# A four-batch decoder kernel: the scan's B rows replicated by SBUF-to-SBUF transfers instead of matmuls and copies, later requests for expert weights, and new interleaving tables

## What is computed

```python
deltaA  = exp(einsum('bld,dn->bldn', delta, A))
deltaBu = einsum('bld,bln,bld->bldn', delta, B, u)
h = h * dA_t + dBu_t                 # over l = 0..255, for each d, n
y = einsum('bdn,bn->bd', h, C_t)     # + u * D afterwards
```

## Time and profile before

| | us |
|---|---|
| median of 3 runs | 985.33 |
| lowest, highest | 984.05, 987.88 |
| the profiled execution's own time | 984.03 |
| its span, first to last instruction | 982.2 |

### The profile page before, as it was taken

How to read it: one execution, slowest core, us unless ns; L and a number is a source line. 1 busy time by engine, 2 the same in 40 slices (tenths; PEclk the granted TensorE clock), 3 DMA queues, 4 the chain that set the end, 5 groups by cost and what they waited for, 6 DMA issues and landing times.

```text
span 982.2 us, 13012 instructions
## 1 busy us (share of the span) xinstructions
PE 870.8 (89%) x4643; PEld 652.0 (66%) x4668; DVE 643.3 (65%) x1378; ACT 383.9 (39%) x828; POOL 358.9 (37%) x393
## 2 busy tenths in 40 slices
PE   6897675988999998889999998888999998789997
PEld 5675344754787786744787886653788786426886
DVE  6332799795355998895355999875355999764333
ACT  4111743326236443426326443417226544243111
POOL 5202485120042875220043875220042876000322
PEclk9897877999999999999999999979999999879999
DMA  6204000002023330301024330302022330300452
GB/s 217 110 0 175 0 1 0 1 14 98 1 81 113 126 113 2 107 29 82 1 81 145 97 111 1 108 1 110 1 68 69 94 109 17 108 1 1 129 153 84
DMA packets 22196, 67.69 MB, mean 69 GB/s; under 512 B 2860, under 2 KB 4780, under 8 KB 21492
## 3 DMA queue, kind: packets, MB, share of 16 engines
q1 hardware_dynamic: 21876, 66.80, 20.8%
q10 hardware_dynamic: 256, 0.07, 0.0%
HBM read 65.74 MB, written 1.05 MB: 68 GB/s over the span
## 4 chain that ended last, share of the span: by engine, by line
PE 49%; DVE 19%; POOL 12%; issue 12%; ACT 7%; DMA 1%; ACTq 1%; POOLq 0%; DVEq 0%; SPq 0%
PE B L779 22%; PE F L779 21%; POOL arena L465 7%; DVE arena L1430 5%; DVE nmx L1501 3%; PE B L1068 3%; POOL spare L550 2%; ACT big L746 2%; POOL arena L475 2%; PE F L808 1%; DVE arena L1270 1%; DVE arena L1442 1%; PE F L790 1%; POOL rs L447 1%; PE B L1149 1%
## 5 line engine op out<-in xcount | busy, mean ns | idle before, releaser
L779 PE MATMUL B<-spare,mw 128*128 128x256 f32 x880 | 209.3, 382 | 0.0
L779 PEld LDWEIGHTS B<-spare,mw 128*128 128x128 f32 x880 | 166.5, 191 | 24.8 <-issue 2.6
L550 POOL TENSOR_TENSOR spare<-q_t 128x256 f32<-128x256 f32 x112 | 82.0, 738 | 193.3 <-DVE q_t L1567 134.2
L1430 DVE TENSOR_TENSOR_SCAN arena<-F,arena 128x512 f32<-128x512 f32 x128 | 149.5, 1207 | 3.7 <-ACT F L702 2.3
L465 POOL TENSOR_TENSOR arena<-du,arena 128x1024 f32<-128x1024 f32 x60 | 140.9, 2360 | 9.8 <-PE F L779 8.5
L702 ACT ACTIVATE F<-delta,a_neg 128x255 f32<-128x255 f32 x256 | 109.9, 467 | 72.6 <-DVE arena L1430 72.6
L779 PE MATMUL B<-mw,spare 128*128 128x256 f32 x448 | 115.4, 381 | 1.2 <-POOL spare L550 1.2
L779 PE MATMUL F<-arena,ident 128*128 128x256 f32 x400 | 105.1, 406 | 1.4 <-POOL arena L475 1.0
L768 ACT ACTIVATE q_t<-B 128x256 f32<-128x256 f32 x112 | 42.0, 381 | 159.2 <-PE B L779 152.6
L1562 DVE SCALAR_TENSOR_TENSOR q_t<-q_t,B 128x256 f32<-128x256 f32 x112 | 46.6, 416 | 77.7 <-ACT q_t L768 77.4
L779 PEld LDWEIGHTS B<-mw,spare 128*128 128x128 f32 x448 | 84.2, 190 | 15.9 <-POOL spare L550 3.9
(11 more groups left out here) (228 smaller groups left out, 1284.0 us busy)
## 6 DMA issues: line engine op xcount, KB each, us to landing
mw<-in_w_moe SPq DMA_DIRECT2D x112, 384.0 KB, 3.1
room<-in_w_f SPq DMA_DIRECT2D x4, 2544.0 KB, 9.1
room<-in_w_l SPq DMA_DIRECT2D x4, 768.0 KB, 7.1
w_m<-in_w_m SPq DMA_DIRECT2D x1, 2112.0 KB
room<-in_w_l SPq DMA_DIRECT2D x4, 512.0 KB, 4.9
x_t<-in_x_t SPq DMA_DIRECT2D x4, 256.0 KB, 3.3
x_tok<-in_x_tok SPq DMA_DIRECT2D x4, 256.0 KB, 6.4
y<-x SPq DMA_DIRECT2D x4, 256.0 KB, 2.2
```

Of the source, the lines that this page charges most:

```text
L550: g.tensor_tensor(hid1[0:r, m % HID_RING, :], hraw[0:r, m % 3, :], crs[0:r, int(m >= MTE), :], ALU.mult)\
L779: return t_.matmul(dst, lhsT, rhs, start=start, stop=stop, skip_group_check=True)
L1430: v.tensor_tensor_scan(h, F[i][:, :], h, 0.0, ALU.mult, ALU.add)\
```

## The change

1. B's rows no longer go through PE and ACT. In a new phase branch `d1` SP waits for ACT's copy of `bct` and issues sixteen transfers, row j of `bct` (1 KB on one partition) to the same half row of `b_rep` on all 128 partitions. Each pair has its own semaphore `rep_in[k]`, and POOL waits for that one where it waited for ACT's copy. PE's and ACT's `replicate` are removed with all their calls.
2. Waits that came with them move: C's first spread now waits for `bcp` and `bct`, the first `sum_states` for `delta0` (bank 3's reader), POOL's step 4 for `dl1`, since `bct` moves from 9472 to 10240 and only `dtr` is left where `hb5` goes.
3. SP asks for expert weights three units later in its own program: in phase `be{m}` it waits for `down{m-3}` and asks for unit m+3.
4. The four tables have new counts.

DVE's split of `bct` into `bcp` stays, since C still needs it.

```diff
-AFTER = {"load": 2, "qkv": 4, "at2": 2, ... "m5": 1, "d2": 2, "d4": 2, "s2": 3, "s3": 1, "s4": 2, "s6": 2, ...
+AFTER = {"load": 2, "qkv": 1, "at0": 1, ... "m5": 1, "d3": 2, "d4": 1, "s0": 2, "s3": 3, "s4": 2, "s6": 3, ...
...
-        dtr, bct, bcr = arena[:, 9216:9472], arena[0:32, 9472:9728], arena[0:32, 9728:9984]
+        dtr, bct, bcr = arena[:, 9216:9472], arena[0:32, 10240:10496], arena[0:32, 9728:9984]
...
+        rep_in = [sem(f"rep_in{k}") for k in range(NK)]
...
+                if ph == "d1":
+                    sp.wait_ge(*af.at("bct", b))
+                    for j in range(NS):
+                        k, half = divmod(j, 2)
+                        sp.dma_start(b_rep[:, k, half * S:half * S + S], bct[j:j + 1, :].unsqueeze(1).to_broadcast([1, P, S]))\
+                            .then_inc(rep_in[k], 16)
...
-                if ph in BE and BE.index(ph) + MW_RING < MT1:
-                    m = BE.index(ph)
+                if ph in BE and 3 <= BE.index(ph) < MT1 - MW_RING + 3:
+                    m = BE.index(ph) - 3
                     sp.wait_ge(*pb.at(f"down{m}", b))
...
                 if dp == 0:
-                    pool.wait_ge(*af.at(f"rep{k}", b))
+                    pool.wait_ge(rep_in[k], b * 32 + 32)
...
+                if n == 4:
+                    pool.wait_ge(*pf.at("dl1", b))
...
-                if ph == "d3":
-                    replicate(b, 0)
...
-                    for k in (1, 2, 3):
-                        replicate(b, k)
...
-                    if ph in STEPS[:2]:
-                        n = STEPS.index(ph)
-                        for k in (4 + 2 * n, 5 + 2 * n):
-                            replicate(b, k)
...
-            def replicate(b, k):
-                act.wait_ge(*pf.at(f"rep{k}", b))
-                copy(b_rep[:, k, :], F[rep_bank(k)][:, :], af, f"rep{k}")
...
-            def replicate(b, k):
-
-                if k == 0:
+            def spread_c(b, n):
+
+                if n == 0:
                     pe.wait_ge(*df.at("bcp", b))
                     pe.wait_ge(*af.at("bct", b))
-                if k == 1:
-                    pe.wait_ge(*af.at("delta0", b))
-                if k >= 2:
-                    pe.wait_ge(*af.at(f"rep{k - 2 if k < 4 else k - 1}", b))
-                spread(F[rep_bank(k)], 2 * k, f"rep{k}")
...
                 if n == 0:
-                    pe.wait_ge(*af.at(f"rep{NK - 1}", b))
+                    pe.wait_ge(*af.at("delta0", b))
...
-                if ph == "d3":
-                    for k in range(3):
-                        replicate(b, k)
-                if ph == "d4":
-                    replicate(b, 3)
```

More of the change, by code:

```diff
@@ L66 @@
              BACK[BACK.index("ba1"):])
[L70 to L77, removed]
[3 rows of a table removed]
-AFTER_DVE = {"load": 2, "at0": 1, "at2": 1, "at3": 2, "at4": 1, "at5": 3, "at6": 1, "at7": 7, "oa": 2, "xa": 1, "xb":
[3 rows of a table removed]
+AFTER = {"load": 2, "qkv": 1, "at0": 1, "at5": 9, "at6": 1, "oa": 11, "xa": 1, "xb": 1, "xc": 3, "xd": 4, "fa1": 1,
+         "fa2": 1, "fa3": 1, "fg1": 1, "fg3": 1, "fg5": 1, "fd1": 2, "m1": 7, "m2": 1, "m5": 1, "d3": 2, "d4": 1,
+         "s0": 2, "s3": 3, "s4": 2, "s6": 3, "s7": 1, "s8": 1, "s9": 1, "s10": 1, "s11": 2, "s14": 1}
+AFTER_POOL = {"load": 1, "qkv": 3, "at2": 16, "at4": 2, "ob": 7, "xa": 2, "xc": 1, "fg1": 1, "fg2": 2, "fg5": 2,
+              "fd1": 5, "fd2": 3, "fd3": 4, "m5": 2, "d3": 1, "d4": 1, "s1": 1, "s2": 1, "s3": 1, "s4": 1, "s5": 3,
+              "s7": 4, "s9": 2, "s10": 1, "s12": 3, "s15": 1}
+AFTER_PE = {"load": 2, "qkv": 1, "at1": 1, "at2": 2, "at3": 2, "at4": 2, "at5": 2, "at6": 4, "at7": 2, "oa": 2, "ob":
[3 rows of a table added]
+AFTER_DVE = {"load": 2, "at0": 1, "at1": 1, "at2": 2, "at3": 2, "at4": 2, "at5": 1, "at6": 5, "at7": 2, "oa": 3, "xb":
+             6, "xc": 4, "xd": 1, "fa1": 3, "fg1": 3, "fg2": 1, "fd1": 5, "fd3": 3, "m1": 1, "m2": 2, "m5": 1, "d3":
+             2, "s1": 1, "s2": 1, "s3": 3, "s4": 1, "s5": 2, "s7": 3, "s8": 1, "s9": 2, "s11": 2, "s12": 1, "u1": 1}
 IDLE_FIRST = {"xa": 7, "fa1": 19}
@@ L346, in state @@
             return hb[:, r, :, :]
-        def rep_bank(k):
-            return 2 if k in (0, 2) else 3
         def max_bank(b, n, i):
@@ L819, in spread @@
                 last.then_inc(pf.step(name), 1)
-            def replicate(b, k):
-                if k == 0:
+            def spread_c(b, n):
+                if n == 0:
                     pe.wait_ge(*df.at("bcp", b))
                     pe.wait_ge(*af.at("bct", b))
-                if k == 1:
-                    pe.wait_ge(*af.at("delta0", b))
-                if k >= 2:
-                    pe.wait_ge(*af.at(f"rep{k - 2 if k < 4 else k - 1}", b))
-                spread(F[rep_bank(k)], 2 * k, f"rep{k}")
-            def spread_c(b, n):
-                if n == 0:
-                    pe.wait_ge(*af.at("rep2", b))
                 else:
@@ L1046, in front @@
                     spread_c(b, n)
-                    if n < 2:
-                        for k in (4 + 2 * n, 5 + 2 * n):
-                            replicate(b, k)
                     if n >= 2:
```

## The result

The changed kernel takes 1204.64 us (median of 4 runs, 1201.76 to 1206.37); the kernel before, run beside it, takes 985.0, and the ratio is 1.226, interval 1.2205 to 1.2314. The forecast was 1247 in a range of 978 to 1320, with 0.69 on slower.

What follows compares the result with a forecast made beforehand. PE, busy 89% of the span, bounds only where it sets the pace; in the scan PE, DVE and POOL are nearly full. 984.03 + 51.3 + 3 x 67.1 + 9 = 1245.6, given as 1247 us for the median; range 978 to 1320.

Steps and rivals of the forecast that it cites:

- The side taken for r: Time r of each one-partition transfer: sixteen DMA engines share a path as wide as one engine's, 4.88 us; chance 0.60.
- 9.76 (k + 1): Batch 0: pair k of B's rows lands this many us, plus 2.2 fixed, after `bct` is written at 106.67.
- first rival: Approach to the scan: transfers run at the issue pace, near 0.46 us, and the removed work counts: 978 us; chance 0.23.
- Batch 0: Scan of batch 0: POOL waits for each pair of rows, step 7 scans at 189.3 instead of 138.01: +51.3 us.
- Batches 1 to 3: PE waits 70 us at `be12` for unit 12's weights queued behind the rows, DVE waits too: +67.1 us a batch.
- the sixteen are all issued by 312.6: Batch 1: SP issues the sixteen transfers in 7.4 us, with unit 12's weights issued just behind.
- The clock: PE after its idle wait in batches 1 to 3: comes back at half clock, 3 us a batch, 9 for three.
- second rival: Scan: transfers are quick and the full DVE hides the removed work, so nothing moves: 985 us; chance 0.08.
- The 6.9 us for the removed work: PE's matmuls and ACT's copies taken out: 0.6 us in batch 0 plus 2.1 in each later batch, the whole gain.
- The tables: Refitted tables let the front come about one expert unit earlier against the back on PE: 0, 5 us either way.
- Free items: SP's later weight request, earlier next-batch transfers, moving `bct` and POOL's wait for `dl1`: taken to cost nothing.

Runs made afterwards that it cites:

- e1: Changed kernel with the sixteen transfers reading all 128 partitions of another tile, B left out of the scan: 984.6 us, ratio 1.0032.
- e8: Changed kernel with all sixteen transfers reading row 0, B's other rows left out: 1234.21 us, measured once.
- e7: Changed kernel with transfers reading 128 partitions of another tile, B left out, and ACT asking for weights of units 6 to 27: 971.02 us, ratio 0.9886.
- e11: Kernel before the change, with ACT asking for the weights of units 6 to 27: 985.57 us, ratio 1.0049.
- e10: Changed kernel with B's rows going through DRAM and the four tables of the kernel before: 985.99 us, ratio 1.0059.
- e2: Kernel before the change, with only the weights asked for three units later in SP's program: 983.92 us, ratio 1.0021.
- e6: Changed kernel with B's rows written to DRAM once and read from there in eight transfers for all partitions: 981.77 us, ratio 0.9992.
- e3: Changed kernel with ACT, on its own queue, asking for the weights of units 6 to 27: 1134.28 us, ratio 1.1552.

## Why the prediction was right, point by point

- **The side taken for r.** Predicted 4.88 us from the engine's own rate, bounds 0.46 and 6.4. Measured 4.81 within a group of four rows, and 4.26 in the mean of sixteen ((177.06 - 106.77 - 2.2) / 16, from POOL's start on the last pair). e1 shows that it is the source and nothing else. The prediction's inference from the Trainium skill ("SBUF — State Buffer", "Door 1: The DMA port swizzle"), that reads too are held to one port's rate, agrees with the trace: 27.2 bytes per ns against 27.2. That page of the Trainium skill does not say which way the transfers of its 27.6 went; "a load" is the prediction's reading. The 435 GB/s of "DMA: Bandwidth & Descriptors" ("Where 436 GB/s comes from") does not describe a copy from one partition, which moved 27 to 30.
- **The term that was mis-sized** is "9.76 (k + 1)" for pair k, 78.1 us for eight. It took no gain where the source passes to a new group of four partitions. The changed kernel does that three times a batch; e8, which never does, has 1234 us. The prediction was 261.6 us above the kernel before, the trace is 221.8 above it, and 64 x (4.88 - 4.26) = 39.7 is the distance between them. That it closes so well is partly luck: `bct` of batch 1 came 3.5 us later than step 7 of batch 0 accounts for (45.0 against 41.5), and each later batch lost 1.3 us less than the sum with 4.26 has (58.9 against 60.2). The range, 978 to 1320, was wide because it had to reach the first rival; that the time lies in it says less than the measured r does.
- **Batch 0.** The first pair was predicted for 118.6; POOL starts at 118.60. Step 7: 189.3 predicted, 179.52 measured, +41.5 in place of +51.3. The 4.26 is read off here, so it is batches 1 to 3 that test it.
- **Batches 1 to 3.** PE at `be12`, C's spread behind it, DVE behind that: as predicted. PE waits 62 us (70 predicted), step 1's product is 58.9 us later against `bct` (66.2 predicted, and 3 more for the clock, which the measured figure holds already); 16 x (4.88 - 4.26) is 9.9 of the difference of 10.3. From output to output (SP's `y<-x` at 503.54 and 783.13) a batch takes 279.6, where it took 219.4.
- **A step that was wrong without harm:** "the sixteen are all issued by 312.6", in 7.4 us of SP. SP took 60 us, since it was held from the third on. Counted from `bct`, the weights were asked for after 60.2 us, not after 7.4. Unit 12 came 71.6 us after `bct` all the same, where the prediction's sum with r = 4.26 gives 2.2 + 68.2 + 0.9 = 71.3: the same transfers had to drain ahead of it either way.
- **The clock.** Predicted 3 us a batch at half speed. PE's restart ran at 0.50 (421 to 427) and unit 12 took 5.3 us from 421.76 to C's spread at 427.04, in place of 2.9: 2.4 us.
- **The first rival's number was wrong.** It let unit 12 land "just as PE gets to it". With quick transfers (e1) PE still waited 5.4 us, three times, and the time was 984.6, not 978. The second rival had the number, but for another reason: e7 shows that the full DVE hides little, since 13.6 us appear when the weights leave SP's queue.
- **The 6.9 us for the removed work** were never measured alone. e7's 0.9886 is about 11 us, with an interval from 5 to 18, and holds the removed work, the new tables and what asking on ACT costs (e11: half a percent).
- **The tables:** put at 0, 5 us either way; e10 puts them at 4 to 7 us of gain.
- **Free items:** the later weight request was rightly put at nothing (e2).

## What to carry to other kernels

Before SBUF is made the source of a broadcast, count how many partitions feed it: what matters is the bytes that leave one small group of partitions, here 27.2 bytes per ns, and DMA engines that are busy at few GB/s are the sign. Fetched for all partitions from DRAM, the same rows were all asked for 5 us after `bct` and landed some 5 us after that (e6), in place of some 70. And a slow or merely numerous set of transfers has to be priced together with what is asked for behind it on the same queue. That was 23 of some 60 us a batch in the changed kernel (e3), and with quick transfers it hid a gain of 13.6 us (e7).

## What the runs showed that was not expected

- SP is held while it issues: 0.53, 0.60, 2.22, then 4.77 us for one transfer. So slow transfers hold up everything behind them in SP's stream, here the request for unit 12's weights by 60 us.
- Issue of a quick 128 KB transfer within SBUF takes 0.64 us in a row of sixteen (10.18 / 16, e1), against 0.46 for the five loads of the earlier trace rows.
- Sources in four or in eight groups in turn give the same 58 GB/s, twice one group's rate; why it stops at two is open.
